# The attention output projection, moved into the last down pass of the feed-forward stage

## What is computed

```python
xn = _layernorm(x, axis=-1)                       # x: (2, 4096, 2048)
# attention: 32 heads of 64, each query sees keys within 64 positions and 16 sinks
qkv = xn @ Wqkv.T + bqkv                          # then rope on q and k
O = softmax([q @ sinks, band(q @ k)]) @ [sinks, v]
s = O @ Wo.T + bo                                 # Wo: 2048 x 2048
# feed-forward: 2048 -> 8192 -> 2048
gate, up = split(xn @ w_gate_up.T)
f = (silu(gate) * up) @ w_down.T
g = silu(f)
out = x + s * g
```

## Time and profile before

| | us |
|---|---|
| median of the timed runs (2) | 2867.97 |
| their range | 2867.48 to 2868.46 |
| profiled execution, its time | 2872.97 |
| profiled execution, span of its slowest core (core 2) | 2871.4 |
| spans of the other cores | 2815.0 to 2859.1 |

### The profile page before, as it was taken

How to read it: one execution, slowest core, us unless ns; L and a number is a source line. 1 busy time by engine, 2 the same in 40 slices (tenths; PEclk the granted TensorE clock), 3 DMA queues, 4 the chain that set the end, 5 groups by cost and what they waited for, 6 DMA issues and landing times.

```text
span 2871.4 us, 32954 instructions; the slowest of 8 cores (2815.0 to 2871.4 us)
## 1 busy us (share of the span) xinstructions
PE 2413.6 (84%) x11736; PEld 1128.2 (39%) x11736; DVE 825.6 (29%) x2481; ACT 549.0 (19%) x1352; POOL 136.7 (5%) x259
## 2 busy tenths in 40 slices
PE   2477777778787878679998999999999999999796
PEld 1143433334343434234444444444444444444343
DVE  5234344443434343421301213021130211203114
ACT  4133333333333333320000000000000000000110
POOL 0000000000000000001001010000101001010000
PEclk9986877777786868679999999999999999999785
DMA  4420111111111011035346261462715436151535
GB/s 134 64 37 19 34 19 34 19 34 19 34 19 37 16 37 19 4 60 94 56 69 108 34 109 34 77 100 45 127 20 84 78 59 118 30 90 35 133 65 205
DMA packets 50749, 173.03 MB, mean 60 GB/s; under 512 B 10144, under 2 KB 11296, under 8 KB 46368
## 3 DMA queue, kind: packets, MB, share of 16 engines
q0 software_dynamic: 41616, 135.03, 28.4%
q1 hardware_dynamic: 8976, 35.90, 3.6%
HBM read 293.34 MB, written 12.58 MB: 107 GB/s over the span
## 4 chain that ended last, share of the span: by engine, by line
PE 61%; DVE 12%; DMA 11%; ACT 8%; issue 5%; DVEq 2%; POOL 1%; SPq 0%; ACTq 0%; POOLq 0%
PE ps_d L849 16%; PE ps_g L823 12%; PE ps_u L835 12%; DMA wd_ib<-wd_pack 8%; PE ps_qk L525 5%; PE ps_s L991 4%; PE ps_qk L512 4%; ACT pB_bf L695 2%; ACT pA_bf L692 2%; DVE m L622 1%; DVE t L618 1%; DVE nmA L631 1%; ACT t2sw L681 1%; ACT t2sw L680 1%; ACT t2sw L678 1%
## 5 line engine op out<-in xcount | busy, mean ns | idle before, releaser
L849 PE MATMUL ps_d<-h_ib,wd_ib 128*128 128x512 bf16 x2048 | 456.0, 386 | 46.7 <-DMA wd_ib<-wd_pack 46.7
L823 PE MATMUL ps_g<-xn_f,gbuf 128*128 128x512 bf16 x2048 | 467.5, 382 | 10.1 <-DMA gbuf<-wgu_pack 10.1
L835 PE MATMUL ps_u<-xn_f,ubuf 128*128 128x512 bf16 x2048 | 465.4, 381 | 0.0
L512 PE MATMUL ps_qk<-xn_f,wx 128*128 128x512 bf16 (+1 forms) x1280 | 312.2, 409 | 32.7 <-DMA wx<-wqkv_pack 28.1
L874 DVE TENSOR_TENSOR h_ib<-tg,ps_u 128x512 bf16<-128x512 f32 x128 | 88.0, 688 | 816.3 <-PE ps_u L835 816.3
L849 PEld LDWEIGHTS ps_d<-h_ib,wd_ib 128*128 128x128 bf16 x2048 | 202.8, 99 | 299.9 <-issue 67.3
L864 ACT ACTIVATE tg<-ps_g 128x512 f32<-128x512 f32 x128 | 76.4, 597 | 1250.7 <-PE ps_g L823 1250.7
L823 PEld LDWEIGHTS ps_g<-xn_f,gbuf 128*128 128x128 bf16 x2048 | 201.4, 98 | 255.2 <-issue 20.7
L835 PEld LDWEIGHTS ps_u<-xn_f,ubuf 128*128 128x128 bf16 x2048 | 201.0, 98 | 243.5 <-issue 8.1
L884 DVE TENSOR_TENSOR g_sb<-g_sb,ps_d 128x512 f32<-128x512 f32 x224 | 153.9, 687 | 284.3 <-PE ps_d L849 284.3
L556 PE MATMUL ps_tp<-id_bf,pA_bf 128*128 128x128 bf16 x128 | 32.0, 250 | 214.1 <-DVE pts_sb L653 158.8
(11 more groups left out here) (94 smaller groups left out, 2006.9 us busy)
## 6 DMA issues: line engine op xcount, KB each, us to landing
gbuf<-wgu_pack POOLq DMA_DIRECT2D x64, 512.0 KB, 5.6
ubuf<-wgu_pack POOLq DMA_DIRECT2D x64, 512.0 KB, 5.8
wd_ib<-wd_pack POOLq DMA_DIRECT2D x64, 512.0 KB, 19.0
wx<-wqkv_pack POOLq DMA_DIRECT2D x32, 512.0 KB, 5.1
u_all<-u_ext SPq DMA_DIRECT2D x9, 1024.0 KB, 18.3
wx<-v_pack POOLq DMA_DIRECT2D x8, 1024.0 KB, 8.9
wobuf<-wo_pack POOLq DMA_DIRECT2D x16, 512.0 KB, 5.1
u_buf<-u_ext SPq DMA_DIRECT2D x8, 1024.0 KB, 7.0
```

Of the source, the lines that this page charges most:

```text
L512: ins = t.matmul(p[:, 0:ln], w[:, kc * 128:(kc + 1) * 128], src[:, kc, :], start=(kc == 0), stop=(kc == 15))
L823: ins = t.matmul(pg[:], gbuf[ic % 2][:, kc * 128:(kc + 1) * 128], xn_f[:, kc, HALO + tsx * 512:HALO + (tsx + 1) * 512], start=(kc == 0), s ...
L835: ins = t.matmul(pu[:], ubuf[ic % 2][:, kc * 128:(kc + 1) * 128], xn_f[:, kc, HALO + tsx * 512:HALO + (tsx + 1) * 512], start=(kc == 0), s ...
L849: ins = t.matmul(pd[:], wd_ib[:, ic, oc * 128:(oc + 1) * 128], h_ib[:, ic, tsx * 512:(tsx + 1) * 512], start=(ic == 0), stop=(ic == 7))
```

## The change

It takes the output projection out of the output stage and puts it into the second half (`tsx` = 1) of the last down pass (`ib` = 7) of the feed-forward stage.

- TensorE: behind the 8 down matmuls of each block `oc` of that half come the wait for `wobuf` and the 2 x 16 projection matmuls of the same block, for both token halves (`tw`).
- ScalarE: behind its last silu of gate come the 32 silu of `g_sb`, each behind the down addition of its block and half and behind the multiply of the one before.
- VectorE: behind each down addition of that half come the two multiplies of the block.
- SP: the load of `o_sb` is issued at the start of the feed-forward stage.
- POOL: the 16 `wobuf` loads stand behind the last `wd_ib` loads. Each waits for the last projection matmul of the block before.
- Memory: `o_sb`, `wobuf` and `gsil` move to the feed-forward stage. `wobuf` and `gsil` become one buffer each, under two names. `ps_s6` moves with them.
- The output stage keeps the `u_buf` loads, transposes, additions and stores, behind the barrier as before.

```diff
@@ feed-forward stage, buffers and SP
+            o_sb = ec(nc.sbuf_tensor("o_sb", [128, 16, 1024], BF16))
+            wobuf = [ec(nc.sbuf_tensor("wobuf0", [128, 2048], BF16))] * 2
+            gsil = [ec(nc.sbuf_tensor("gsil0", [128, 512], F32))] * 2
...
+            def p5_sync(s):
+                OS_outer[0].wait_all(s)
+                OSB.dma(s, o_sb[:], d_oscr.rearrange("a p b -> p a b"))
+            block.sync(p5_sync)
@@ counts
                         cVS += 1; vs_ge[(ib, tsx, oc)] = cVS
+                        if ib == 7 and tsx == 1:
+                            for tw in range(2):
+                                cTS += 1; ts_s6[(oc, tw)] = cTS
+                                cSS += 1; ss_gs[(oc, tw)] = cSS
+                                cVS += 1; vs_sg[(oc, tw)] = cVS
@@ p5_gp
                     assert tok == wdtok[ib]
+                for oc in range(16):
+                    if oc >= 1:
+                        ctx.wait(g, "TS", ts_s6[(oc - 1, 1)])
+                    tok = WO.dma(g, wobuf[0][:], d_wo[oc], oc % 2)
+                    assert tok == wotok[oc]
@@ p5_tensor
                             ctx.inc(ins, "TS")
+                            if ib == 7 and tsx == 1:
+                                WO.wait(t, wotok[oc])
+                                if oc == 0:
+                                    OSB.wait_all(t)
+                                for tw in range(2):
+                                    jw = oc * 2 + tw
+                                    if jw >= 2:
+                                        ctx.wait(t, "VS", vs_sg[(oc - 1, tw)])
+                                    pw = ps_s6[jw % 2]
+                                    for kc in range(16):
+                                        ins = t.matmul(
+                                            pw[:], wobuf[0][:, kc * 128:(kc + 1) * 128],
+                                            o_sb[:, kc, tw * 512:(tw + 1) * 512],
+                                            start=(kc == 0), stop=(kc == 15))
+                                    ctx.inc(ins, "TS")
@@ p5_scalar
+                    if ib == 7:
+                        for oc in range(16):
+                            for tw in range(2):
+                                jw = oc * 2 + tw
+                                ctx.wait(sc, "VS", vs_ge[(7, tw, oc)])
+                                if jw >= 1:
+                                    pv = ((jw - 1) // 2, (jw - 1) % 2)
+                                    ctx.wait(sc, "VS", vs_sg[pv])
+                                ctx.inc(sc.activation(gsil[0][:],
+                                                      g_sb[:, oc, tw * 512:(tw + 1) * 512],
+                                                      AF.Silu), "SS")
+                                sc.drain()
@@ p5_vector
                             ctx.inc(ins, "VS")
+                            if ib == 7 and tsx == 1:
+                                for tw in range(2):
+                                    jw = oc * 2 + tw
+                                    dstw = g_sb[:, oc, tw * 512:(tw + 1) * 512]
+                                    ctx.wait(v, "TS", ts_s6[(oc, tw)])
+                                    ctx.wait(v, "SS", ss_gs[(oc, tw)])
+                                    ctx.inc(v.scalar_tensor_tensor(
+                                        dstw, ps_s6[jw % 2][:], bo_pc[:, oc:oc + 1],
+                                        gsil[0][:], OP.add, OP.mult), "VS")
@@ output stage
-            o_sb = ed(nc.sbuf_tensor("o_sb", [128, 16, 1024], BF16))
-            wobuf = [ed(nc.sbuf_tensor(f"wobuf{i}", [128, 2048], BF16)) for i in range(2)]
-            gsil = [ed(nc.sbuf_tensor(f"gsil{i}", [128, 512], F32)) for i in range(2)]
...
             def p6_sync(s):
-                OS.wait_all(s)
-                OSB.dma(s, o_sb[:], d_oscr.rearrange("a p b -> p a b"))
                 for tt in range(NT_OWN):
...
-            def p6_gp(g):
-                for oc in range(16):
-                    if oc >= 2:
-                        ctx.wait(g, "TS", ts_s[(oc - 2, 1)])
-                    tok = WO.dma(g, wobuf[oc % 2][:], d_wo[oc], oc % 2)
-                    assert tok == wotok[oc]
-            block.gpsimd(p6_gp)
```

More of the change, by code:

```diff
@@ L753, in build_program2 @@
             WD = Slots(nc, glob, "wd", 1)
+            WO = Slots(nc, glob, "wo", 2)
+            OSB = Slots(nc, glob, "osb", 1)
+            def p5_sync(s):
+                OS_outer[0].wait_all(s)
+                OSB.dma(s, o_sb[:], d_oscr.rearrange("a p b -> p a b"))
+            block.sync(p5_sync)
             base = dict(ctx.cnt)
@@ L758, in build_program2 @@
             wdtok = [None] * 8
+            wotok = [None] * 16
             ts_gt = {}
@@ L764, in build_program2 @@
             vs_ge = {}
+            ts_s6 = {}
+            ss_gs = {}
+            vs_sg = {}
             cTS, cSS, cVS = base["TS"], base["SS"], base["VS"]
@@ L768, in build_program2 @@
             wdc = 0
+            woc = [0, 0]
+            for oc in range(16):
+                woc[oc % 2] += 16; wotok[oc] = (oc % 2, woc[oc % 2])
             for ib in range(8):
@@ L893, in build_program2 @@
                         for i in range(2)]
+                ps_s6 = [sP5.enter_context(nc.psum_tensor(f"ps_s6{i}", [128, 512], F32))
+                         for i in range(2)]
                 block.tensor(p5_tensor)
@@ L971, in p6_sync @@
                 OUT.wait_all(s)
-            def p6_gp(g):
-                for oc in range(16):
-                    if oc >= 2:
-                        ctx.wait(g, "TS", ts_s[(oc - 2, 1)])
-                    tok = WO.dma(g, wobuf[oc % 2][:], d_wo[oc], oc % 2)
-                    assert tok == wotok[oc]
-            block.gpsimd(p6_gp)
-            def p6_tensor(t):
[L982 to L994, removed]
+            def p6_tensor(t):
                 for tt in range(NT_OWN):
@@ L997, in p6_tensor @@
                         j6 = tt * 16 + oc
-                        if j6 == 0:
-                            ctx.wait(t, "VS", vs_sg_all)
                         if j6 >= 2:
@@ L1005, in p6_tensor @@
                                             id_f[:]), "TS")
[L1007 to L1015, removed]
             def p6_vector(v):
@@ L1019, in p6_vector @@
                     DBG.wait_all(v)
[L1020 to L1028, removed]
                 for tt in range(NT_OWN):
@@ L1040, in build_program2 @@
             with ExitStack() as sP6:
-                ps_s6 = [sP6.enter_context(nc.psum_tensor(f"ps_s6{i}", [128, 512], F32))
-                         for i in range(2)]
                 ps_tr6 = [sP6.enter_context(nc.psum_tensor(f"ps_tr6{i}", [128, 128], F32))
@@ L1046, in build_program2 @@
                 block.tensor(p6_tensor)
-                block.scalar(p6_scalar)
                 block.vector(p6_vector)
-                assert ctx.cnt["TS"] == cTS and ctx.cnt["SS"] == cSS
-                assert ctx.cnt["VS"] == cVS
+                assert ctx.cnt["TS"] == cTS and ctx.cnt["VS"] == cVS
             if _DEBUG:
@@ L1056, in build_program2 @@
                 block.sync(dmp6)
-    return nc
+        return nc
 def _prep_inputs(L0_attn_u, L0_attn_Wqkv, L0_attn_bqkv, L0_attn_Wo, L0_attn_bo,
```

2 lines of the change are left out of this document (removed).

## The result

| | before | after |
|---|---|---|
| median of the timed runs, us | 2853.57 (10 runs) | 2937.14 (11 runs) |
| ratio of the time after to the time before | | 1.0285 (95%: 1.0258 to 1.0313) |
| profiled execution, its time, us | 2872.97 | 2929.62 |
| spans of the 8 cores, us | 2815.0 to 2871.4 | 2877.0 to 2927.9 |

A forecast was written before the change was run, and what follows sets the result against it. TensorE's own stream plus one exposed o_sb load was taken to bound the kernel. 2871.4 - 24.6 + 62.3 + 34.8 + 7.2 + 5 - 7.8 = 2948.3 us of span, 2944.9 timed; range 2905 to 2985.

The forecast's parts named there:

- waits for wobuf: Merged stage: TensorE idles 4.15 us at each of 15 bare reloads of the single weight buffer, +62.3 us.
- clock after each idle: Merged stage: the granted clock drops after each reload idle, 2.32 us each, 15 times, +34.8 us.
- hole and restart: Before the projection: the 22.0 us wait for o_sb closes and the 2.6 us half-clock restart goes, -24.6 us.
- first gbuf later: Start of the feed-forward stage: the o_sb load beside the first weight loads delays the first gbuf, +5 us.
- bare u_buf: Start of the tail: the u_buf load, formerly under the projection, is issued only after the barrier, +7.2 us.
- gsil single: Merged stage: one gsil buffer costs nothing while ScalarE and VectorE lie beside the 3.45 us matmul groups.
- lower clock of 0.81 to 0.87: Projection on cores 2 and 3: half of the 15.6 us lost to the lower clock comes back, -7.8 us.
- Rival 1: Each restart in the merged stage: the clock stays up, so no clock cost; 2910 us, chance 0.16.
- Rivals 2 and 3: Wobuf reloads: 2, landing of some 3.2 us, 2882 us, chance 0.04; 3, wholly hidden under down group, 2848, chance 0.02.
- Rival 4: Wobuf reloads: loads land late, core 3's 8.06 us in all blocks, +44.4 us; 2989 us, chance 0.13.
- Rival 5: Start of the feed-forward stage: early o_sb load gives back its saving, +14 for +5; 2954 us, inside the forecast.

The follow-up runs named there:

- 16 fillers: Changed kernel with 16 filler matmuls of unused result after the down group of each block from 1 on; ratio to the kernel before 1.0215.
- the merged kernel: Changed kernel with two weight buffers, later o_sb load, half a u_buf tile loaded early: 0.9912; with wd_ib loads spread and o_sb later still: 0.9735.
- the run without cover: Changed kernel with TensorE's wait for wobuf put ahead of the block's down group, so nothing lies over the reload; ratio to the kernel before 1.0503.
- the unmerged, repaired kernel: Kernel before with o_sb loaded after the first gate and up groups, first two wobuf loads ahead of the barrier into gate weight buffers; ratio 0.9936.

## Why the prediction held

Forecast 2945 us, range 2905 to 2985, slower by over 2% with 0.73. Measured 2937.14. By its steps, with the merged stage as the measure:

| step | predicted, us | measured, us | from |
|---|---|---|---|
| waits for wobuf | +62.3 | +61.7 on core 6 (61.4 to 63.3 over the cores) | page and waits after |
| clock after each idle | +34.8 | +31.4, or 29 by filling the idle | stage less waits; 16 fillers |
| hole and restart | -24.6 | -22.0 for the hole; the restart, not measured by itself, taken at 2.6 | no wait for o_sb is left |
| first gbuf later | +5 | +5.6 (10.1 on core 2 before, 15.7 on core 6 after); +4.5 in the mean of the cores | pages and waits |
| bare u_buf | +7.2 | +7.1, the bare load; the tail as a whole grew by 7.9, from core 2 to core 6, and 5.2 in the mean of the cores | chain after; spans less projection |
| gsil single | 0 | 0 | order of time |
| lower clock of 0.81 to 0.87 | -7.8 | none left | below |

The measured terms without the last sum to +81, against the 83.6 us between the two medians. Between the two profiled executions the spans differ by only 56.5 us. There the 15.6 us that core 2 had lost to the lower clock fall away, and core 6 waited 6.3 us less for wd_ib (40.4 for 46.7): 81.2 - 15.6 - 6.3 = 59.3. The first step held to 1%: the path of a reload was read on one instance, the landing from 16, and both repeated 15 times.

The clock term was right in its mechanism and its size: it took the mean of 1.69 and 2.95 us per idle, and after idles of 4.1 us both amounts came back, the smaller 75 times in 120 and the larger 45 times. But the rule beside it (a loss after 4.23 us, none after 2.74) is not how it goes. At 2.4 us of idle the same reading would have said 0 where 12 to 17 were measured. The trace of the kernel before could have told: of its five idles of 2.0 to 3.0 us ahead of a down pass, those on cores 0, 1 and 5 cost nothing, and those on cores 6 and 7 cost 1.7 us each. On core 6:

```profile
2058.41 57.10 PE L849 MATMUL ps_d<-h_ib,wd_ib 128*128 128x512 bf16 x251 [2.15 <-DMA wd_ib<-wd_pack]
```

That the idle here came out at 4.1 us, where every idle costs, kept this from mattering. Rival 1 (the clock stays up) is refuted by the granted clock of 0.85 over the stage.

The one step that failed is the last, the 7.8 us taken back for the lower clock of cores 2 and 3. The prediction set its sum against an execution in which core 2 had lost 15.6 us of the projection to a granted clock of 0.81 to 0.87 and took half of it back. In the profile after that clock is absent from the merged stage, and the kernel before itself mostly runs faster than that execution. What was read as a property of the projection was one of that execution, and of two of its cores. On the other six its 512 matmuls took 112.6 to 115.4 us with their waits for wobuf, where core 2 took 128.6. Core 1:

```profile
2670.20:2782.80 112.60, 112.10 (x512) 50.07 (x512) 23.26 (x31) 18.88 (x30) 7.40 (x14) 0.99 0.42 77
```

Set against the later median of 2853.57, the other terms alone give 2853.6 + 84.7 = 2938.3. The starting point was 14.4 us too high and the failed term took back 7.8 of them; the 6.6 us left are most of the 7.8 by which the forecast lay above 2937.14. That these two errors ran against each other is luck. What sets this clock off stays open.

Rivals 2 and 3 are refuted (no wobuf landing under 4.9 us). Rival 4 didn't happen: the median landing is 5.0 or 5.1 us on all cores, also on core 3, which had 6.2. Rival 5's 14 us didn't either: the longest first gbuf wait is 15.7 us, 5.1 above the longest before.

What the prediction did not see is that the early o_sb load is only half of what closes the hole. By itself it gave nothing, since the next load stood in the same place; the changed kernel gains the whole hole because it moves the first wobuf load ahead as well. And the prediction took the slowest core's waits for wd_ib as given, though without them the cores ended within 17 us of each other and not 51: loads spread over the stage brought 1.4% alone (0.7 to 2.2%), and took the merged kernel from 0.9912 to 0.9735, where all other repairs together had brought 0.9%.

## What to carry to other kernels

Before a double buffer is given up for memory, price the reload as issue + landing + restart less what runs beside it, times the number of reloads, and add the clock that each idle costs, which for short idles is a share of them and not a threshold; here a free buffer of the finished stage would have done. A load moved out of a hole uncovers the one that hid beside it: look for every transfer issued behind the same barrier. Large weight loads issued in one burst can set the slowest core; spread them over the stage that hides them.

## What the runs showed of the hardware

- Whether a short idle of TensorE costs the upper clock level did not follow from its length alone. Of 120 idles per kernel in the merged stage, none of 0.7 us was followed by slower matmuls, 56 of about 2.4 us were, 101 of about 3.3 us, and all of 4.1 us; each that cost took 1.2 to 1.7 us or 2.2 to 2.9 us. Idles that stand alone, ahead of a down pass, go the same way over all profiles of this case: of 108 under 1.9 us none cost, of 72 between 1.9 and 3.0 us 47 cost 1.7 us each, and all 305 of 4.0 us and more cost.
- A granted clock of 0.81 came and went without a change in the kernel's work, mostly on two cores at a time. In the kernel before it stood over most of the projection on cores 2 and 3, and over 72 us of the first 270 us on cores 0 and 1. In the run without cover it stood for 161 us of the feed-forward stage on cores 0 and 1, while core 2 had 1.00 there. In the changed kernel's profile it stood for 6 to 8 us at the start of the feed-forward stage on cores 4 to 7, and in the other profiles it does not occur. What sets it off stays open.
- The same program waited between 4.7 and 48.2 us for wd_ib on different cores of one execution (cores 3 and 1 of the unmerged, repaired kernel).
